# A new order of stages on all five engines of a two-layer transformer kernel

## The chip, the core and the metric

The kernel runs on one core of one Trainium2 chip. The metric is the device time of one execution in microseconds (us), as the median of several runs. Five engines run side by side, each taking its own instructions strictly in order: PE (TensorE, matrix products), ACT (ScalarE), DVE (VectorE), POOL (GpSimd) and SP (SyncE, which here only issues DMAs). They meet through semaphores.

## The reference

The input is 2 x 1024 rows of 256 features. With LN for a layer norm without weights, the reference computes

```
xn = LN(x);  x = x + attention0(xn) + ffn0(xn)
xn = LN(x);  x = x + attention1(xn) + ffn1(xn)
```

- attention0: causal attention over 1024 positions, 32 query heads and 8 key/value heads of 8 dimensions, with rotary position coding and biases.
- ffn0: gated GELU with fp8 operands, 256 to 2 x 1024 to 256.
- attention1: for each position, attention among its 16 heads of 16 dimensions, with a rotary coding.
- ffn1: gated SiLU, an RMS norm over 1024, and ternary weights that are quantized from the fp32 weights in groups of 64.

## The kernel before

The rows are cut into 16 tiles of 128, eight for each of the two sequences. For a tile n the work is a set of named stages, and each stage has a function on the engine that does it:

- **Front of attention0.** `ln0`, `rs0` (POOL), `xn`, then on PE `xnT` (transpose) and `qkv` (projection), `qkvc` (DVE), `rope`, `qr`, `q2` (POOL), `qh`, `qm` (ACT) and `q0`, `q1` (DVE), which split q and k into pieces of bf16, `qxT` (PE transposes) and `kTc`, `qTc` (DVE copies).
- **Quads.** A quad Q is one block of 128 keys for one half of the heads of a tile. There are 144 quads. `qk.Q` writes four banks of scores (`psS`), `exp.Q` is four activations of 128x512 that empty them into `Pt`, `mask.Q` (POOL) is run on diagonal blocks, and `pv.Q` sums into `psV`. `qk.Q+1` needs the banks that `exp.Q` has read. `S1` and `ex1` of the second attention use the same four banks.
- **Back of attention0.** `ob`, `obT`, `att`, `attT`, `attTc`, `wo0`, `xa`.
- **ffn0.** four `up` per tile, `g`, `fh`, `sq`, `th` (ACT), `ge1`, `ge3` (DVE), `down`, `yff`, `xf`.
- **Front of attention1.** `ln1`, `rs1`, `xn1`, `xn1T`, `xn1Tc`, two `qkv1` per tile, `qk1c`, `ro1`, `ro2`, `v1c`. Then SP writes the tile to memory (`vw`) and reads it back in another layout (`vr`, three DMAs into the single buffer `G3`), and PE transposes it twice (`gT`). `vr.n` waits until `PV1.n-1` has read `G3`.
- **attention1.** `gTq` (DVE), `gTk` (ACT), `S1`, `ex1` (ACT), `PV1`, `o1r`, `o1T`, `o1`; `ow` and `at1r` (SP) carry the result through memory, `at1T`, `at1Tc`, `wo1`, `yo`.
- **ffn1.** four `gu` per tile, `tg` (ACT), `sg`, `hh` (DVE), `ssq` (ACT), `ssm`, `rsg`, `hxa` (ACT), `hx` (DVE), two `hxT`, `hTc`, `dn1`, `yout`, and `out` (SP).
- **Weights.** `w8` casts the fp8 weights. `tc`, `ts`, `tsc`, `tm`, `tcs`, `td`, `tde`, `tr`, `tw` do the ternary quantization in six blocks. `sin` and `tab` make the angles of the second rotary coding. `vz`, `idc`, `cst`, `zero`, `gz` fill constants.

Nothing on the chip chooses the order of the work. A table `ORDER` (lines 45 to 183) holds one string per engine, and each engine walks its string and calls the stage functions:

```
for name, n in first_pass("pe"):
    run[name](n)
```

Every stage begins with its waits, `w.wait_ge(semaphore, count)`, whose counts follow from the stage number alone. An engine that stands at a wait runs nothing that is behind it in its string.

All PE stages other than `qk`, `pv` and `S1` write to one of three shared banks, psA, psB and psC, in rotation (`shared`). The bank is given by the place of the stage in the order of fills: a fill takes the bank of the third fill before it, and waits until that one has been emptied by the stage that `EMPTIED` names. There are 500 fills. So the order on PE also says which bank a stage gets and whose copy it waits for.

Of the kernel before, what the change touches and what calls it, by code (L numbers as in the profile page):

```python
# [46 lines left out]
        "xnT.0 qkv.0 xnT.1 ts.0 qkv.1 ts.1 qxT.0 qxT.1 qxT.2 qk.0 qk.1 td.0 up.0 up.1 xnT.2 qxT.3 pv.0 qkv.2 qxT.4 "  # L47
        "xnT.3 pv.1 qxT.5 obT.0 tr.0 up.2 qk.2 attT.0 qkv.3 up.3 td.1 up.4 qk.3 pv.2 up.5 qk.4 pv.3 qk.5 down.0 "
        "qxT.6 tr.1 qxT.7 up.6 qxT.8 up.7 pv.4 pv.5 qk.6 wo0.0 ts.2 up.8 ts.3 qk.7 pv.6 up.9 qxT.9 qxT.10 qk.8 pv.7 "
        "qxT.11 td.2 xnT.4 qk.9 td.3 tr.2 pv.8 pv.9 qk.10 tr.3 down.1 qkv.4 ts.4 obT.1 ts.5 qk.11 pv.10 attT.1 up.10 "  # L50
        "up.11 qk.12 wo0.1 up.12 td.4 qk.13 td.5 tr.4 up.13 tr.5 xnT.5 pv.11 xn1T.0 qkv.5 ts.6 obT.2 pv.12 qk.14 "
        "pv.13 attT.2 ts.7 qxT.12 qk.15 pv.14 down.2 qxT.13 qk.16 wo0.2 td.6 qxT.14 td.7 tr.6 qk.17 pv.15 pv.16 tr.7 "
        "qkv1.0 qkv1.1 ts.8 qk.18 ts.9 qxT.15 gu.0 up.14 qk.19 pv.17 pv.18 td.8 up.15 td.9 tr.8 up.16 tr.9 up.17 "
        "qk.20 pv.19 up.18 ts.10 down.3 ts.11 obT.3 up.19 qxT.16 qk.21 attT.3 xnT.6 pv.20 qk.22 pv.21 wo0.3 td.10 "
        "qk.23 td.11 tr.10 qxT.17 pv.22 qk.24 pv.23 tr.11 qkv.6 down.4 gu.1 qk.25 pv.24 gu.2 gu.3 qk.26 pv.25 xnT.7 "
        "xn1T.1 qk.27 pv.26 qkv1.2 gT.0 gT.1 qk.28 pv.27 S1.0 hxT.0 qkv1.3 hxT.1 qk.29 PV1.0 pv.28 qk.30 qxT.18 "
        "o1T.0 qxT.19 gu.4 qxT.20 qk.31 pv.29 gu.5 obT.4 gu.6 qk.32 at1T.0 attT.4 pv.30 wo0.4 wo1.0 gu.7 dn1.0 qk.33 "
        "pv.31 pv.32 qkv.7 qk.34 pv.33 xn1T.2 gT.2 gT.3 qk.35 pv.34 qkv1.4 qkv1.5 gu.8 gu.9 qk.36 pv.35 gu.10 gu.11 "
# [1585 lines left out]
```

## Time and profile before

| | us |
|---|---|
| median of 3 runs (684.7 to 686.87) | 685.07 |
| the profiled execution, its own time | 683.55 |
| its span, first to last instruction | 681.8 |
| PE busy | 609.7 (89%) |
| ACT busy | 502.1 (74%) |
| DVE busy | 450.6 (66%) |
| POOL busy | 279.4 (41%) |

The profiled execution is 1.5 us under the median. Its own time is 1.75 us above its span. The granted TensorE clock had a mean of 0.98 of full speed. A busy share says how long an engine ran something. It does not say what set the end; for that the waits of each stretch must be read.

### The profile page before, as it was taken

What the parts mean: (1) busy time and instruction counts of PE and PEld (TensorE: products, weight loads), DVE (VectorE), ACT (ScalarE), POOL (GpSimd) and SP (SyncE); (2) the same over time, 40 slices, a digit from 0 to 9 for tenths busy, and PEclk for the clock granted to TensorE, in tenths of its full rate; (3) what the DMA queues carried; (4) which work ended last, traced back from release to release, by engine and by line L of the source; (5) the groups of instructions that cost most, each with busy time, mean ns of one, the idle gap of its engine ahead of it and who ended that gap; (6) DMA issues with size and microseconds to landing.
All of it is one profiled execution on the core that took longest, in us unless ns stands there. A gap on an engine that the chain in (4) does not pass through costs nothing.

```text
span 681.8 us, 13961 instructions
## 1 busy us (share of the span) xinstructions
PE 609.7 (89%) x5206; PEld 305.7 (45%) x5245; DVE 450.6 (66%) x901; ACT 502.1 (74%) x941; POOL 279.4 (41%) x415
## 2 busy tenths in 40 slices
PE   2688988997999999999999998989999979998873
PEld 1244433443434455454545345654345524444552
DVE  5897988976556676847888965555537725536653
ACT  2559988985688986888789787478999848875330
POOL 6668575172333133634888561103144222312100
PEclk9999999999999999999999999999999979999997
DMA  8511010034000412312100114151021120043620
GB/s 280 197 56 32 32 32 1 1 48 63 9 24 24 63 19 38 39 18 47 40 1 1 47 19 57 29 80 30 25 25 17 39 39 25 25 70 40 91 42 20
DMA packets 150921, 30.47 MB, mean 45 GB/s; under 512 B 133952, under 2 KB 149568, under 8 KB 150848
## 3 DMA queue, kind: packets, MB, share of 16 engines
q1 hardware_dynamic: 150272, 29.19, 21.5%
q8 instruction: 43, 0.70, 0.4%
q10 hardware_dynamic: 576, 0.33, 0.2%
q14 instruction: 30, 0.25, 0.1%
HBM read 19.02 MB, written 10.49 MB: 43 GB/s over the span
## 4 chain that ended last, share of the span: by engine, by line
PE 46%; DMA 7%; DVE 6%; issue 3%; SPq 3%; ACT 2%; POOL 1%; DVEq 0%; POOLq 0%
PE psV L651 11%; PE psS L636 6%; DMA G<-qkvscr 3%; SPq L487 3%; DMA oscr<-o 2%; PE psS L754 2%; PE psB L819 2%; PE psC L800 2%; DMA at<-oscr 2%; PE psA L819 1%; PE psA L800 1%; PE psB L800 1%; ACT stage L935 1%; PE psC L765 1%; PE psA L765 1%
## 5 line engine op out<-in xcount | busy, mean ns | idle before, releaser
L887 ACT ACTIVATE Pt<-psS 128x512 f32<-128x512 f32 x576 | 300.0, 626 | 61.6 <-PE psS L636 43.0
L651 PE MATMUL psV<-Pt,vaug 128*32 128x512 f32 x1152 | 152.4, 611 | 1.7 <-POOL Pt L1507 1.0
L1507 POOL TENSOR_SCALAR_AFFINE_SELECT Pt<-Pt 128x512 f32<-128x512 f32 x128 | 86.9, 713 | 62.8 <-ACT Pt L887 62.6
L636 PE MATMUL psS<-qT,kT 49*128 49x512 bf16 x576 | 94.6, 388 | 4.7 <-ACT Pt L887 2.7
L636 PEld LDWEIGHTS psS<-qT,kT 49*128 49x128 bf16 x576 | 21.5, 94 | 63.4 <-ACT Pt L887 28.5
L651 PEld LDWEIGHTS psV<-Pt,vaug 128*32 128x32 f32 x1152 | 24.8, 109 | 51.2 <-issue 45.9
L935 ACT ACTIVATE stage<-psS 128x512 f32<-128x512 f32 x64 | 33.1, 606 | 15.9 <-PE psS L754 15.7
L1562 POOL TENSOR_TENSOR ss<-ss,mhalf 128x1 f32<-128x1 f32 x16 | 8.9, 554 | 79.9 <-DVE ss L1343 79.9
L1543 POOL TENSOR_TENSOR xhs<-xn1T,xhs 128x256 f16<-128x256 f32 x16 | 11.7, 729 | 52.8 <-DVE xhs L1260 52.8
L1208 DVE SCALAR_TENSOR_TENSOR gw<-gw,gb 128x512 f32<-128x512 f32 x32 | 24.7, 781 | 10.4 <-ACT gw L901 10.4
L1553 POOL TENSOR_TENSOR r<-qk,cos 128x256 f32<-128x256 f32 x16 | 14.6, 909 | 41.4 <-ACT qk L919 32.5
L1527 POOL TENSOR_TENSOR yfb<-yff,bo 128x256 f32<-128x256 bf16 x16 | 12.8, 799 | 45.3 <-DVE yff L1235 45.3
L1349 DVE SCALAR_TENSOR_TENSOR qtmp<-qtmp,ss 128x1024 f16<-128x1024 f32 x16 | 22.3, 1396 | 10.1 <-ACT qtmp L955 10.0
L950 ACT ACTIVATE qtmp<-qtmp 128x1024 bf16<-128x1024 f32 x16 | 17.2, 1073 | 13.9 <-issue 6.0
L1536 POOL TENSOR_SCALAR rs<-mv 128x1 f32<-128x1 f32 x16 | 6.2, 386 | 48.5 <-DVE mv L1243 48.5
L1217 DVE SCALAR_TENSOR_TENSOR ga<-gw,gb 128x512 bf16<-128x512 f32 x32 | 24.4, 763 | 1.1 <-ACT gw L912 1.0
L800 PE MATMUL psA<-wguT,xhs 128*128 128x512 bf16 x89 | 23.2, 380 | 0.9 <-issue 0.5
L912 ACT ACTIVATE gw<-gw 128x512 f32<-128x512 f32 x32 | 21.1, 668 | 3.2 <-DVE gw L1208 3.2
L1490 POOL TENSOR_TENSOR rt<-rt,QX 128x320 f32<-128x320 f32 x16 | 14.7, 916 | 20.2 <-ACT QX L873 15.8
L800 PE MATMUL psB<-wguT,xhs 128*128 128x512 bf16 x75 | 20.5, 390 | 1.9 <-issue 1.3
L754 PE MATMUL psS<-qk1T 24*128 24x128 f32 x512 | 20.8, 284 | 1.1 <-ACT qk1T L926 1.1
L901 ACT ACTIVATE gw<-gb 128x512 f32<-128x512 bf16 x32 | 21.4, 695 | 0.1
(355 smaller groups left out, 1363.2 us busy)
## 6 DMA issues: line engine op xcount, KB each, us to landing
qkvscr<-rqkv SPq DMA_DIRECT2D x16, 384.0 KB, 2.7
G<-qkvscr SPq DMA_DIRECT2D x48, 128.0 KB, 3.7
stage<-in_wg SPq DMA_DIRECT2D x4, 512.0 KB, 6.4
oscr<-o SPq DMA_DIRECT2D x16, 128.0 KB, 3.2
at<-oscr SPq DMA_DIRECT2D x16, 128.0 KB, 2.0
out<-yout SPq DMA_DIRECT2D x16, 128.0 KB, 1.7
x<-in_x SPq DMA_DIRECT2D x1, 1536.0 KB, 11.8
r<-in_wgu SPq DMA_DIRECT2D x2, 512.0 KB, 8.6
```

The lines of the kernel that those rows point to most:

```text
L636: e.matmul(psS[j][:], kT[64 * f:64 * f + 49, j, 128 * at:128 * at + 128], qd[64 * f:64 * f + 49, 4 * j:4 * j + 4, :].rearrange("p s n -> p ...
L651: ins = e.matmul(psV[32 * j:32 * j + 32, :], vaug[:, at, j, 32 * f:32 * f + 32], Pt[(4 * Q + j) % NP][:], start=(kb == 0 and h == 0), stop ...
L754: ins = e.matmul(psS[b][:, 128 * j:128 * j + 128], qk1T[32 * b:32 * b + k, 1, j, :], qk1T[32 * b:32 * b + k, 0, j, :], start=True, stop=True)
L800: ins = e.matmul(bank[:], src[:, pt, 128 * c:128 * c + 128], wguT[:, c, c0:c0 + 512], start=(k == 0), stop=(k == 3))
L887: e.activation(Pt[u % NP][:], psS[j][:], ACT.Exp, scale=SC0).then_inc(S["exp"], 1)
L901: e.activation(gw[:, half, :], gb[:, half, :], ACT.Square).then_inc(S["sq"], 1)
L912: e.activation(gw[:, half, :], gw[:, half, :], ACT.Tanh, scale=GC * GA).then_inc(S["th"], 1)
L935: e.activation(P1[:, 4 * b:4 * b + 4, :].rearrange("p g n -> p (g n)"), psS[b][:], ACT.Exp, scale=SC1).then_inc(S["ex1"], 1)
L1208: e.scalar_tensor_tensor(gw[:, half, :], gw[:, half, :], 1.0 / GA, gb[:, half, :], ALU.add, ALU.mult).then_inc(S["ge1"], 1)
L1217: e.scalar_tensor_tensor(a, gw[:, half, :], 1.0, gg, ALU.add, ALU.mult).then_inc(S["ge3"], 1)
L1349: e.scalar_tensor_tensor(hx_b[:, 1, :], h1, sn[:, 2:3], hx_b[:, 0, :], ALU.mult, ALU.subtract).then_inc(S["hx"], 1)
L1507: e.affine_select(out=p, in_=p, pattern=[[0, 4], [1, 128]], compare_op=ALU.is_ge, fill=0.0, base=0, channel_multiplier=-1).then_inc(S["mas ...
```

## The change

The five strings of `ORDER` are replaced. Each engine still runs exactly the same stages (804 on PE, 435 on ACT, 670 on DVE, 178 on POOL and 88 on SP), with the same functions and the same wait counts. 60 stages on PE, 47 on ACT, 18 on DVE, 18 on POOL and 25 on SP keep their place in the string. Since the place of a fill on PE gives its bank, the banks of the shared fills change with it. The core of the diff, the parts that the prediction speaks of:

```diff
     "pe": (
-        "xnT.0 qkv.0 xnT.1 ts.0 qkv.1 ts.1 qxT.0 qxT.1 qxT.2 qk.0 qk.1 td.0 up.0 up.1 xnT.2 qxT.3 pv.0 qkv.2 qxT.4 "
...
-        "xn1T.1 qk.27 pv.26 qkv1.2 gT.0 gT.1 qk.28 pv.27 S1.0 hxT.0 qkv1.3 hxT.1 qk.29 PV1.0 pv.28 qk.30 qxT.18 "
-        "o1T.0 qxT.19 gu.4 qxT.20 qk.31 pv.29 gu.5 obT.4 gu.6 qk.32 at1T.0 attT.4 pv.30 wo0.4 wo1.0 gu.7 dn1.0 qk.33 "
...
-        "hxT.21 qxT.47 qk.122 pv.121 o1T.10 qkv1.23 qk.123 down.15 pv.122 qk.124 pv.123 gu.44 qk.125 pv.124 at1T.10 "
...
-        "gu.55 o1T.12 gu.56 pv.143 gT.26 gT.27 obT.15 S1.13 gu.57 attT.15 gu.58 at1T.12 wo0.15 gu.59 wo1.12 PV1.13 "
-        "dn1.12 xn1T.15 hxT.26 o1T.13 qkv1.30 gT.28 gT.29 qkv1.31 S1.14 gu.60 hxT.27 PV1.14 at1T.13 o1T.14 gu.61 "
-        "gu.62 gu.63 gT.30 gT.31 S1.15 at1T.14 wo1.13 wo1.14 dn1.13 hxT.28 PV1.15 hxT.29 o1T.15 dn1.14 hxT.30 hxT.31 "
-        "at1T.15 wo1.15 dn1.15"),
+        "xnT.0 qkv.0 ts.0 xnT.1 xnT.2 ts.1 qkv.1 qxT.0 xnT.3 qxT.1 qxT.2 qkv.2 up.0 up.1 qk.0 up.2 qxT.3 qxT.4 qkv.3 "
+        "qk.1 qxT.5 td.0 td.1 qk.2 pv.0 up.3 tr.0 up.4 pv.1 qk.3 pv.2 tr.1 xnT.4 qxT.6 qxT.7 qk.4 obT.0 qxT.8 ts.2 "
...
+        "down.4 up.21 qxT.19 qxT.20 pv.29 qk.31 gu.4 o1T.0 pv.30 pv.31 qk.32 hxT.1 gu.5 gu.6 qk.33 gu.7 pv.32 qk.34 "
+        "obT.4 gu.8 pv.33 pv.34 qk.35 qkv1.4 qk.36 at1T.0 gT.2 qxT.21 pv.35 qk.37 pv.36 wo1.0 attT.4 qk.38 gT.3 "
...
+        "gT.26 gT.27 obT.15 gu.56 attT.15 S1.13 wo0.15 gu.57 PV1.13 gu.58 at1T.12 gu.59 xn1T.15 o1T.13 wo1.12 "
+        "qkv1.30 qkv1.31 gT.28 gT.29 hxT.26 S1.14 dn1.12 PV1.14 hxT.27 at1T.13 o1T.14 gu.60 wo1.13 gu.61 gu.62 "
+        "dn1.13 gT.30 gT.31 hxT.28 S1.15 gu.63 at1T.14 hxT.29 PV1.15 o1T.15 wo1.14 dn1.14 hxT.30 hxT.31 dn1.15 "
+        "at1T.15 wo1.15"),
     "act": (
-        "tc.0 sin.0 qh.0 qm.0 qh.1 exp.0 qm.1 exp.1 tde.0 g.0 fh.0 sq.0 th.0 g.1 exp.2 qh.2 sq.1 fh.1 qm.2 g.2 th.1 "
...
+        "tc.0 qh.0 qm.0 qh.1 g.0 qm.1 sq.0 fh.0 g.1 th.0 exp.0 sq.1 exp.1 tde.0 qh.2 tde.1 exp.2 g.2 sq.2 fh.1 qm.2 "
...
+        "sq.6 exp.14 th.6 sin.0 g.7 sq.7 fh.7 exp.15 tde.6 tde.7 exp.16 g.8 fh.8 qh.5 tc.4 qk1c.0 qm.5 exp.17 tg.0 "
...
     "dve": (
-        "vz.0 idc.0 ln0.0 xn.0 ln0.1 xnTc.0 ln0.2 xn.1 ln0.3 cst.0 qkvc.0 tab.0 xnTc.1 va.0 q0.0 w8.0 qkvc.1 q1.0 "
...
+        "ln0.0 vz.0 xn.0 ln0.1 ln0.2 xnTc.0 xn.1 ln0.3 idc.0 xn.2 qkvc.0 tsc.0 va.0 w8.0 xnTc.1 xnTc.2 tsc.1 q0.0 "
+        "w8.1 qkvc.1 xn.3 q1.0 tm.0 w8.2 kTc.0 xnTc.3 va.1 qTc.0 w8.3 qTc.1 q0.1 tcs.0 q1.1 qkvc.2 w8.4 va.2 ge1.0 "
...
     "pool": (
-        "zero.0 gz.0 rs0.0 rs0.1 rs0.2 rs0.3 rope.0 qr.0 q2.0 rope.1 qr.1 mask.0 q2.1 rs0.4 mask.1 rs0.5 rope.2 qr.2 "
...
+        "zero.0 rs0.0 rs0.1 rs0.2 rope.0 rs0.3 qr.0 q2.0 rope.1 qr.1 q2.1 rope.2 mask.0 mask.1 qr.2 rs0.4 q2.2 "
```

## Rows read from the trace of the kernel before

**Rows 1.** Page: span, busy time and share, granted clock by slices
```profile
span 681.8 us, 13961 instructions
PE 609.7 (89%) x5206; PEld 305.7 (45%) x5245; DVE 450.6 (66%) x901; ACT 502.1 (74%) x941; POOL 279.4 (41%) x415
PEclk9999999999999999999999999999999979999997
```

**Rows 2.** Busy time of each engine in five stretches: stretch, length, PE, PEld, DVE, ACT, POOL, clock
```profile
0.00:27.00 27.00, 10.09 (x34) 5.44 (x34) 16.71 (x43) 6.43 (x8) 15.68 (x34) 1.00 0.87 294
27.00:175.00 148.00, 130.67 (x975) 60.19 (x990) 121.39 (x229) 119.80 (x221) 83.74 (x121) 0.99 0.14 32
175.00:540.00 365.00, 352.90 (x3206) 179.84 (x3220) 241.65 (x485) 301.32 (x574) 153.19 (x221) 1.00 0.19 31
540.00:618.00 78.00, 73.04 (x572) 30.94 (x578) 34.96 (x69) 57.02 (x109) 22.06 (x33) 0.96 0.23 42
618.00:681.80 63.80, 42.99 (x423) 29.30 (x424) 35.88 (x78) 17.52 (x29) 4.73 (x8) 0.89 0.33 50
```

**Rows 3.** Waits of PE from 27 to 618 us: total, times, longest
```profile
PE psB L550 <- DMA at<-oscr: 6.0, 3, 3.8
PE psA L550 <- DMA at<-oscr: 4.6, 1, 4.6
PE psB L721 <- DMA G<-qkvscr: 2.8, 3, 1.6
PE psS L636 <- ACT Pt L887: 2.7, 2, 2.0
PE psC L721 <- DMA G<-qkvscr: 1.7, 1, 1.7
```

**Rows 4.** Chain that ended last, 440 to 475 us: start, us, what
```profile
448.65 1.85 PE psV L651 x16
472.72 0.54 PE psS L636 x4
473.26 0.99 PE psV L651 x8
```

**Rows 5.** Timeline of PE around at1T.0: start, us, instruction, idle before
```profile
169.40 0.33 PE L550 MATMUL psA<-identf,at 128*128 128x128 f32 x1 [4.59 <-DMA at<-oscr]
170.02 1.94 PE L651 MATMUL psV<-Pt,vaug 128*32 128x512 f32 x8
```

**Rows 6.** Timeline of ACT, table loads and the first exponential
```profile
11.94 1.28 ACT L851 ACT_TABLE_LOAD   x1
18.58 0.26 ACT L851 ACTIVATE sin<-ang 128x64 f32<-128x64 f32 x1 [5.36 <-DVE ang L1001]
28.15 1.28 ACT L887 ACT_TABLE_LOAD   x1
29.45 2.07 ACT L887 ACTIVATE Pt<-psS 128x512 f32<-128x512 f32 x4
```

**Rows 7.** Busy time of each engine in the slice from 68 us
```profile
68.20:102.30 34.10, 30.73 (x224) 13.52 (x220) 30.79 (x59) 30.74 (x58) 22.25 (x30) 1.00 0.10 32
```

**Rows 8.** Timeline of PE in the tail: pv.143, PV1.14, S1.15, o1T.15, at1T.15, dn1.15
```profile
618.88 1.07 PE L651 MATMUL psV<-Pt,vaug 128*32 128x512 f32 x8
641.87 1.08 PE L765 MATMUL psB<-stage,G 128*32 128x128 f32 x32 [0.78 <-ACT stage L935]
652.66 1.17 PE L754 MATMUL psS<-qk1T 24*128 24x128 f32 x32 [0.78 <-ACT qk1T L926]
659.96 0.66 PE L774 MATMUL psB<-identf,o1r 128*128 128x128 f32 x4 [0.26 <-DVE o1r L1312]
666.43 0.33 PE L550 MATMUL psC<-identf,at 128*128 128x128 f32 x1 [1.17 <-DMA at<-oscr]
668.47 3.47 PE L819 MATMUL psB<-wpT,stmp 128*128 128x256 bf16 x16
```

**Rows 9.** Timeline of DVE and ACT in the tail: last yout, ssq.15
```profile
671.97 0.42 DVE L1379 TENSOR_TENSOR yout<-psB,yo 128x256 f32<-128x256 f32 x1 [2.84 <-PE psB L819]
659.78 1.06 ACT L950 ACTIVATE qtmp<-qtmp 128x1024 bf16<-128x1024 f32 x1 [3.83 <-issue]
```

241 rows, old and new, of the table ORDER are left out of this document.

## Prediction

> **What bounds the kernel now.** I read the page first, then the busy times by stretch, then PE's waits, then the chain that ended last, and only then timelines of the places where PE stood. The page says that PE is busy 89% of the span and ACT 74% [rows 1], so PE is the engine whose idle time counts. The stretches say where it idles [rows 2]: 16.9 us of the first 27, 17.3 us of the next 148, only 12.1 us of the 365 after that, 5.0 us from 540 to 618, and 20.8 us of the last 63.8. The reader is to see that the middle is nearly full and that the head, the first quarter and the tail are not. The order matters only where PE stands still or runs its matmuls at the lower clock.
>
> PE's waits from 27 to 618 us name the cause there [rows 3]: 10.6 us for the DMA that brings `at1` back (`at1T`) and 4.5 us for the DMA that fills `G3` (`gT`), 15.1 us together. The next one, scores that wait for `exp`, is 2.7 us. Two of the waits are long, 4.6 us before `at1T.0` and 3.8 us before `at1T.10`. What follows such a wait is slow too: the `pv` behind `at1T.0` took 1.94 us [rows 5], against 0.99 for one in a dense stretch [rows 4]. So a wait of 4.6 us cost PE nearly another 1 us in that `pv` alone.
>
> **The change, part by part.** No instruction is added or removed in the text of the stages, so each term is a wait that goes, one that comes, or work that moves under something else.
>
> *Round trips through memory in the middle.* I counted, in the two PE strings, the work that lies between `o1T.n` and `at1T.n`, weighing each stage with its slot at full clock (0.54 us for a `qk`, 0.99 for a `pv` [rows 4], and likewise for the others, between 0.25 and 1.8). For `at1T.0` before, this is qxT, gu, qxT, qk, pv, gu, obT, gu, qk, or 6.0 us. Behind the new order stand 13.8 us. Over the sixteen tiles, fifteen gaps before are 7.3 us or shorter, and fifteen after are 8.3 us or longer. The trip itself is short when nothing else is in the way: from the end of `o1T.15` (659.96 + 0.66 = 660.6) to `at1T.15` at 666.4 it is 5.8 us [rows 8]. The same count between `PV1.n-1` and `gT.2n` gives seven gaps of 3.3 to 5.2 us before and none under 6.4 after. So the new order covers both trips in nearly every tile. If all of the 15.1 us [rows 3] went, and with them some 3.5 us of slow matmuls behind the waits (my estimate from four slots like the one in [rows 5], each 0.65 to 1.0 us over its dense length), the gain would be 18.6 us. The other bound is 0: in a program with in-order queues a wait that is covered often shows up at the next late copy. The work that is now put between producer and consumer has to be ready too, and ACT and DVE are busy for 80% and more of the second stretch [rows 2]. I take a little over half, **-10 us**, because the middle has other slack (DVE 66%, ACT 83% of the third stretch) but the second stretch has not.
>
> *Tail.* Before, the last `pv` ends at 619.9, `S1.15` starts at 652.7 and the last `yout` ends at 672.4: 32.8 and 19.7 us [rows 8, 9]. In the new string the projection `qkv1.30 qkv1.31` stands directly behind `wo1.12`, no longer behind `dn1.12`, and not split by `gT.28 gT.29`. Counting slots and the copies between them from `pv.143` on, I get `qkv1.31` some 5 us earlier, and `PV1.14` ending 20 us after `pv.143` in place of 23 (641.87 + 1.08 = 642.95 [rows 8]). `vr.15` waits for `PV1.14`; with some 6 us for the trip, `gT.30` can run at 26 and `S1.15` at 27.4 instead of 32.8, 5.4 us earlier. Behind `S1.15` the old string has `at1T.14 wo1.13 wo1.14 dn1.13 hxT.28` ahead of `PV1.15`, 5.4 us after `S1.15` starts, while `ex1.15` is done after 3.3. The new one has `gu.63 at1T.14 hxT.29`, so `PV1.15` starts at about 3.3. `hxT.29` also releases `ssq.15`, which began only at 659.8 [rows 9], 7.1 us after `S1.15`. And `dn1.15` now comes ahead of `at1T.15`. In the old order it ran last and alone, at the lower clock, in 3.47 us [rows 8]. My count of this last piece gives 15.0 to 16.6 us where 19.7 stood, the second value with `dn1.15` still slow. Together that is 8.5 to 10.1 us. It needs ACT and DVE to be prompt, which they can be: they are busy for 17.5 and 35.9 us of these 63.8 [rows 2]. As lower bound I keep 3, the gain behind `S1.15` alone. I take **-8 us**. The checks behind the last `yout`, some 9 us to the end of the span, are the same.
>
> *Head.* `sin` no longer stands between `tc.0` and `qh.0`; there ACT waited 5.36 us for the angles [rows 6]. `gz` goes out of the way of `rs0.0`, and `cst` and `tab` out of the way of the copy of the first projection. Each of the first steps becomes ready 1 to 2 us earlier. But `w8.1` to `w8.3`, `tm.0` and two `up` now come ahead of `qk.0`, and by my count `qk.0` starts where it did, at about 27 us, with `qkv.2`, `xnT.2`, `xnT.3`, `up.0` and `up.1` done (2.7 us of slots more). I take **-2 us**, with +1 if the weights land later than counted and -5 if the second stretch profits as well.
>
> *Sine in the busy stretch.* `sin.0` now stands between `th.6` and `g.7`, behind `exp.14`. Its own two activations are 0.5 us. A load of 1.28 us preceded `sin` and another the first exponential [rows 6]; now the tanh and exponentials on both sides want a table other than that of `sin`, so I count two loads there, 2 x 1.28 + 0.5 = 3.1 us of ACT, in the slice where ACT is busy for 30.7 of 34.1 us [rows 7]. That is the upper bound, 0 the lower, if PE has other work. I take **+1.5 us**. The Trainium skill speaks against this move more strongly (ScalarE: Activation LUTs, What ACT_TABLE_LOAD costs): every switch to another set costs the load and a drain of the same length, some 2.66 us. By that page the move would cost ACT 5.8 us and the sum would be 1.3 us higher. The trace does not show such a drain: the exponential starts at 29.45, right behind the load that began at 28.15 and lasted 1.28 [rows 6].
>
> *Pairs.* Two adjacent `pv` take 1.85 us where two single ones take 1.98 [rows 4]. The number of such neighbours on PE rises from 17 to 38, which is worth at most 21 x 0.13 = 2.7 us; stages that alternate between fp32 and narrower operands cost a little and rise from 405 to 416. I take **-1 us** (bounds 0 and -2.7).
>
> The sum is -10 - 8 - 2 + 1.5 - 1 = -19.5 us. Against the profiled execution's own 683.55 this gives 664.05; the median of the runs stands 1.5 us above that execution, so I predict **665.6 us**.
>
> **Rivals.** *All of it comes* (chance 0.17): every covered wait is really gone, 18.6 in place of 10, tail 10, head 3, pairs 2, no cost for the sine: 683.55 - 33.6 + 1.5 = about 651, and up to 659 if one of them falls short. For it speaks the regularity of the new gaps; against it that ACT and DVE fill up where PE does.
>
> *Only the ends come* (0.20): the waits for the two DMAs go, but PE then waits for copies and exponentials at the same pace, since the second stretch is held by ACT. Then tail and a part of the head remain, 5 to 11 us, or 671 to 682, about 677. For it speaks that the 12.1 us of idle in the third stretch are spread thinly.
>
> *Nothing changes* (0.05): every gain is handed back; 683 to 687.
>
> *Slower, by the three shared banks* (0.08): each of the 497 fills behind the first three waits for the copy of the third fill before it. I counted the PE work between the two: it is under 1.5 us for 98 fills before and for 119 after. Where DVE has something else ahead of that copy (one more 128x512 operation is 0.7 us), PE stands. If the new DVE string meets the short gaps 0.3 us worse on average, 119 x 0.3 = 36 us come back, and the kernel runs at 685 - 19.5 + 36 = about 701. This decides from 0.17 us per short gap on (20/119). Against it: the fewest-slack gaps, below 1.2 us, fall from 55 to 49.
>
> **How the numbers follow.** The forecast, 659 to 671, has a chance of 0.50. The range reaches into the rivals on both sides, down to 655 and up to 679; outside lie half of the first rival and a good part of the last three, 0.2 in all. A change of less than 0.3% (2 us) can't be told from none in this kernel. Faster by more than that: 0.50 + 0.17 + 0.20 = 0.87. Within it: 0.05. Slower: 0.08.
>
> **What the changed profile would show.** PE's waits from the first quad to `pv.143` would have at most 3 us for the DMAs of `at1` and `G3` together, and no `pv` of 1.9 us. `pv.143` would end near 610. From its end to `S1.15` would be 27 to 30 us, and from there to the last `yout` 15 to 17. ACT would have four table loads, two of them around `sin` near 85 us, each with no more than 0.1 us of idle behind it. I would be wrong by the second rival if PE's idle in the second and third stretch stayed near 29 us with other names in the list of waits, and by the last if waits of psA, psB and psC for DVE grew by more than 10 us.

## The result and the profile after

| | before | after |
|---|---|---|
| median of the runs, us | 684.88 (4 runs, 684.34 to 686.87) | 646.5 (4 runs, 643.59 to 648.37) |
| ratio | | 0.9431, 95% interval 0.9386 to 0.9476 |
| the profiled execution, its own time | 683.55 | 643.59 |
| span | 681.8 | 641.8 |
| PE busy, idle | 609.7, 72.1 | 592.7, 49.1 |

The new order is 38.4 us faster. That is twice what was forecast (19.5), and below the range. The profiled executions differ by 40.0 us, which is the number that the readings below add up to; the one of after is the fastest of its four. The page of after answers to [rows 1]:

```profile
span 641.8 us, 13919 instructions
PE 592.7 (92%) x5195; PEld 304.4 (47%) x5245; DVE 437.3 (68%) x901; ACT 498.0 (78%) x941; POOL 275.3 (43%) x415
PEclk9799999999999999999999999999999999999997
```

PE's idle time fell by 23.0 us and its busy time by 17.0, though it runs the same instructions. A reader who looks only at the idle time misses much of the gain. The split is not exact: these two traces lack records of matmuls (5206 and 5195 of the 5245 that there are, most of the missing ones `gu`, 28 and 41), and a missing record shows as idle time or lengthens its neighbour. Where a split between busy and idle matters below, two traces that have all 5245 decide. The busy time by stretch answers to [rows 2] (columns: stretch, length, then PE, PEld, DVE, ACT, POOL, clock, DMA share, GB/s):

```profile
0.00:27.00 27.00, 10.99 (x39) 5.89 (x40) 16.14 (x40) 5.00 (x6) 15.55 (x31) 0.91 0.88 300
27.00:175.00 148.00, 136.31 (x1074) 62.00 (x1086) 124.62 (x238) 135.05 (x254) 90.39 (x129) 0.99 0.14 31
175.00:500.00 325.00, 321.29 (x2930) 167.03 (x2955) 213.14 (x443) 272.06 (x523) 134.93 (x203) 1.00 0.21 34
500.00:578.00 78.00, 77.02 (x648) 35.82 (x653) 43.16 (x93) 65.97 (x128) 25.73 (x40) 1.00 0.20 35
578.00:641.80 63.80, 47.10 (x514) 33.69 (x513) 40.19 (x90) 19.94 (x34) 8.71 (x14) 0.93 0.38 62
```

From 27 to 175 us PE idles 11.7 us where it idled 17.3, and ACT is busy for 135.1 us where it was for 119.8: it does more of its work early, and the stretch that I took to be held by ACT got shorter even so. From 175 to 500 the idle time is 3.7 us, from 500 to 578 it is 1.0. The waits of PE from 27 us to the last `pv` answer to [rows 3] (total, times, longest). These are the largest; no wait for the DMAs of `at1` or `G3` is in the list:

```profile
PE psA L599 <- POOL QX L1501: 1.5, 1, 1.5
PE psC L566 <- DVE qkv L1100: 1.2, 1, 1.2
PE psV L652 <- POOL Pt L1508: 0.8, 2, 0.6
PE psB L567 <- DVE qtmp L1052: 0.8, 2, 0.5
```

PE around `at1T.0` ([rows 5] before, with 4.59 us of idle and a `pv` of 1.94 us behind it). There is no idle in brackets now, and what follows the first `pv` starts 1.00 us behind it, the second `pv` 0.54 behind the `qk`, both dense:

```profile
170.45 0.33 PE L551 MATMUL psB<-identf,at 128*128 128x128 f32 x1
...
171.47 1.06 PE L652 MATMUL psV<-Pt,vaug 128*32 128x512 f32 x8
172.47 0.61 PE L637 MATMUL psS<-qT,kT 49*128 49x512 bf16 x4
173.01 1.07 PE L652 MATMUL psV<-Pt,vaug 128*32 128x512 f32 x8
```

ACT's table loads ([rows 6]) and `sin`, now in the busy stretch:

```profile
2.76 1.28 ACT L859 ACT_TABLE_LOAD   x1 [2.76 <-issue]
...
91.13 1.28 ACT L852 ACT_TABLE_LOAD   x1
92.42 0.26 ACT L852 ACTIVATE sin<-ang 128x64 f32<-128x64 f32 x1
...
94.56 1.28 ACT L888 ACT_TABLE_LOAD   x1
95.86 1.57 ACT L888 ACTIVATE Pt<-psS 128x512 f32<-128x512 f32 x3
```

The tail on PE and DVE answers to [rows 8, 9]: the last `pv` (two in one record), `S1.15`, `dn1.15`, `at1T.15`, the last `yout`:

```profile
585.08 1.92 PE L652 MATMUL psV<-Pt,vaug 128*32 128x512 f32 x16
616.64 1.17 PE L755 MATMUL psS<-qk1T 24*128 24x128 f32 x32 [0.33 <-DVE qk1T L1296]
627.39 1.91 PE L820 MATMUL psC<-wpT,stmp 128*128 128x256 bf16 x16 [1.36 <-DVE yout L1380]
629.14 0.27 PE L551 MATMUL psA<-identf,at 128*128 128x128 f32 x1
```
```profile
631.72 0.42 DVE L1380 TENSOR_TENSOR yout<-psC,yo 128x256 f32<-128x256 f32 x1
```

From the end of the last `pv` (587.0) to `S1.15` are 29.6 us (32.7 before), from there to the end of the last `yout` (632.1) 15.5 (19.7 before). `dn1.15` takes 1.91 us and no longer 3.47, since the granted clock is 1.00 there until 633 us; in the old order it was 0.5 from 668.2 to 671.6.

**Three stretches tell the whole difference.** Cut both executions at the first quad and at the end of the last `pv`. Before, and then after:

```profile
0.00:27.10 27.10, 10.09 (x35) 5.48 (x36) 16.81 (x43) 6.43 (x8) 15.78 (x34) 1.00 0.87 294
27.10:619.95 592.85, 558.56 (x4762) 271.31 (x4798) 399.01 (x785) 479.68 (x907) 259.01 (x375) 0.99 0.18 33
619.95:681.80 61.85, 41.05 (x410) 28.92 (x413) 34.76 (x74) 15.98 (x27) 4.61 (x8) 0.89 0.31 49
```
```profile
0.00:30.00 30.00, 13.99 (x58) 7.59 (x58) 18.56 (x43) 5.91 (x7) 17.11 (x32) 0.89 0.87 293
30.00:587.00 557.00, 540.61 (x4727) 268.92 (x4772) 384.35 (x784) 475.78 (x908) 253.81 (x377) 1.00 0.19 33
587.00:641.80 54.80, 38.12 (x414) 27.92 (x417) 34.35 (x75) 16.34 (x27) 4.38 (x7) 0.92 0.34 60
```

The first quad starts 2.9 us later, but 3.9 us more of PE's work lies ahead of it, so the head gives 1.0. The tail gives 7.05. (The start of the first quad differs between executions of one and the same head: 26.0 to 29.1 us in the ten traces with the old one, middle 26.9, and 30.0 to 32.4 in the eight with the new one, middle 31.6. The 30.0 is the earliest of its kind. By the middles the new head starts the quads 4.7 us later with some 4 us more work done, which is no gain.) The stretch between is 35.85 us shorter: 17.9 of idle and 17.95 of busy time, 3.9 of the latter being the work that moved ahead. What the other 14 us of busy time are, and which part of the order took the idle time away, the experiments have to tell.

One part stands in the clock. In the old order the granted clock fell to half (1.2 of 2.4 GHz) three times in this stretch, each time at a wait of PE for one of the two DMAs: the wait of 4.59 us that ended at 169.40, one of 1.74 for `G3` that ended at 425.95, and the one of 3.81 that ended at 550.44. Before, the three stretches:

```profile
169.90:173.30 3.40, 3.40 (x13) 1.38 (x12) 0.76 (x2) 1.21 (x3) 0.00 (x0) 0.50 0.00 0
425.90:429.30 3.40, 3.35 (x15) 2.19 (x15) 1.12 (x2) 1.72 (x3) 0.00 (x0) 0.50 0.35 65
548.80:555.60 6.80, 5.16 (x18) 1.21 (x18) 1.11 (x2) 2.07 (x4) 1.52 (x3) 0.50 0.14 25
```

PE is busy for 11.9 us of them at half pace, which costs an estimated 6 us. After, the granted clock is 1.00 from 29 to 633 us. (The 1.00 of the first row of before counts the time ahead of the first record of the clock as full; `qk.0` at 27.09 us took 1.03 us and one behind `at1T.0` in the new order 0.61, so the clock was low there too.)

### The profile page after: what moved, and what is told of

It is laid out like the page before. It is cut to its first block and busy times, and to the rows that moved or that the text cites. A ratio compares the mean times of both kernels' runs of the same rounds, so it can differ in the third digit from the quotient of the medians.

```text
span 641.8 us, 13919 instructions
## 1 busy us (share of the span) xinstructions
PE 592.7 (92%) x5195; PEld 304.4 (47%) x5245; DVE 437.3 (68%) x901; ACT 498.0 (78%) x941; POOL 275.3 (43%) x415
## 5 line engine op out<-in xcount | busy, mean ns | idle before, releaser
L888 ACT ACTIVATE Pt<-psS 128x512 f32<-128x512 f32 x576 | 298.5, 621 | 37.8 <-PE psS L637 29.7
L652 PE MATMUL psV<-Pt,vaug 128*32 128x512 f32 x1152 | 146.1, 601 | 1.8 <-POOL Pt L1508 0.8
L1508 POOL TENSOR_SCALAR_AFFINE_SELECT Pt<-Pt 128x512 f32<-128x512 f32 x128 | 87.5, 721 | 54.7 <-ACT Pt L888 54.5
L637 PE MATMUL psS<-qT,kT 49*128 49x512 bf16 x576 | 96.7, 382 | 1.8 <-ACT Pt L888 0.5
L652 PEld LDWEIGHTS psV<-Pt,vaug 128*32 128x32 f32 x1152 | 26.5, 108 | 54.6 <-issue 41.7
L1477 POOL TENSOR_TENSOR rt<-qkv,cs 128x320 f32<-128x320 f32 x16 | 14.9, 930 | 37.4 <-DVE qkv L1100 36.8
L1218 DVE SCALAR_TENSOR_TENSOR ga<-gw,gb 128x512 bf16<-128x512 f32 x32 | 26.4, 824 | 4.6 <-ACT gw L913 4.6
L874 ACT ACTIVATE QX<-rt 128x768 bf16<-128x768 f32 x16 | 14.0, 876 | 15.0 <-PE psB L599 9.5
L1500 POOL TENSOR_TENSOR QX<-rt,QX 128x256 bf16<-128x256 f32 x16 | 12.0, 750 | 29.7 <-ACT QX L880 22.3
L1209 DVE SCALAR_TENSOR_TENSOR gw<-gw,gb 128x512 f32<-128x512 f32 x32 | 23.3, 729 | 0.8 <-ACT gw L902 0.8
L1544 POOL TENSOR_TENSOR xhs<-xn1T,xhs 128x256 f16<-128x256 f32 x16 | 12.5, 782 | 26.1 <-DVE xhs L1261 26.1
L801 PE MATMUL psB<-wguT,xhs 128*128 128x512 bf16 x84 | 22.2, 379 | 1.3 <-issue 0.6
L1221 DVE TENSOR_TENSOR ga<-ga,fb 128x512 bf16<-128x512 bf16 x32 | 18.7, 586 | 5.1 <-ACT fb L908 1.5
L1480 POOL TENSOR_TENSOR rt<-qkv,sn 128x160 f32<-128x160 f32 x32 | 22.1, 713 | 0.0
L951 ACT ACTIVATE qtmp<-qtmp 128x1024 bf16<-128x1024 f32 x16 | 17.3, 1079 | 5.5 <-issue 5.5
```

The source lines that it names most:

```text
L637: e.matmul(psS[j][:], kT[64 * f:64 * f + 49, j, 128 * at:128 * at + 128], qd[64 * f:64 * f + 49, 4 * j:4 * j + 4, :].rearrange("p s n -> p ...
L652: ins = e.matmul(psV[32 * j:32 * j + 32, :], vaug[:, at, j, 32 * f:32 * f + 32], Pt[(4 * Q + j) % NP][:], start=(kb == 0 and h == 0), stop ...
L801: ins = e.matmul(bank[:], src[:, pt, 128 * c:128 * c + 128], wguT[:, c, c0:c0 + 512], start=(k == 0), stop=(k == 3))
L888: e.activation(Pt[u % NP][:], psS[j][:], ACT.Exp, scale=SC0).then_inc(S["exp"], 1)
L1209: e.scalar_tensor_tensor(gw[:, half, :], gw[:, half, :], 1.0 / GA, gb[:, half, :], ALU.add, ALU.mult).then_inc(S["ge1"], 1)
L1218: e.scalar_tensor_tensor(a, gw[:, half, :], 1.0, gg, ALU.add, ALU.mult).then_inc(S["ge3"], 1)
```

## The experiments

Each median stands beside runs of the kernel before on the same chip (medians 683.4 to 684.9 us). "Trips" are the two ways through memory, `ow` and `at1r` to `at1T`, and `vw` and `vr` to `gT`.

### One third of the order at a time

Three kernels take the new order on all five engines for a part of the work and the old one for the rest. They are cut at `qk.30` and `pv.138` in PE's string, and each other engine at what these need.

```diff
 e1: -[old to qk.30]  +[the same stages in new order]   [old from there]
 e2:  [old to qk.30]            -[old to pv.138]  +[new order]    [old from there]
 e3:  [old to pv.138]           -[old to the end] +[new order]
```

Head alone (e1):

> The stages that the old order runs up to qk.30 (with the copies that empty their banks) stand in the relative order of the new one; all later stages stand as in the old order. If the gains of the stretches simply add up, this gives what the new kernel had gained at qk.30, 5 to 7 us. If the new head only pays because of what the new middle does with it, the gain is under 3 us.

683.72 us, ratio 0.999 (0.9962 to 1.0018): no change to be seen. In the trace it is 3.1 us ahead at `qk.30`, and then loses them at the cut. PE's waits from 150 to 195 us:

```profile
PE psB L595 <- POOL QX L1497: 4.6, 1, 4.6
```

Middle alone (e2):

> Only the stages from qk.30 to pv.138 stand in the relative order of the new string; head and tail are old. If the gains add up, the middle alone gives 23 to 28 us. If the middle's gain needs the head's (work that crosses the cut), it is under 18 us.

668.08 us, ratio 0.9758 (0.971 to 0.9806). At `qk.138` it is 26.0 us ahead, and from there to `qk.143` it needs 29.3 us where 17.4 stood before. 6.6 of the 12 us lost at this cut are two waits. Waits of PE from 560 to 620 us:

```profile
PE psB L718 <- DMA G<-qkvscr: 6.6, 2, 4.4
```

Tail alone (e3):

> Only the stages behind pv.138 stand in the new relative order. By the count of the tail the gain is 6 to 9 us; if the tail's latency is the DMAs' own, under 3 us.

680.08 us (10 runs), ratio 0.9936 (0.9908 to 0.9964). The middle holds most of the gain, the tail 4.7 us by the medians and 7.35 in the traces (61.85 to 54.5 us from the last `pv` to the end). The profiled execution of this kernel was the fastest of its ten, 5.3 us under their median. A spliced order costs something at its cut, so these three are rather lower bounds.

### The trips in the old order

In the first kernel (e4) `at1T.n` transposes the result of tile n-1, so that it never waits for its own trip; in the second (e5) `gT` transposes a constant weight as well. All DMAs are still issued, but the second attention's output goes to the wrong tile, and with `gT` changed its scores are made from other numbers.

```diff
-                w.wait_ge("d_or", 16 * (n + 1))
-                transpose_pair(shared("at1T", n), at1[n % len(at1)], "at1T")
+                w.wait_ge("d_or", 16 * n)
+                transpose_pair(shared("at1T", n), at1[(n + 1) % 2], "at1T")
...
-                w.wait_ge("d_vr", 48 * (n + 1))
-                transpose_groups(shared("gT", m), s, "gT")
+                w.wait_ge("d_c", 96)
+                ins = e.transpose(bank[:, 128 * j:128 * j + 128], wo0_w[...], identf[:])
```

> The old order, but at1T transposes the attention result that came back for the tile before (a second buffer, zeros for tile 0), so its output is left wrong in the second attention; all DMAs and stages remain, and only the wait for the tile's own round trip is gone. Theory 1, a covered wait is gone for good and takes the slow matmuls behind it along: 12.4 us of waits and 2 to 5 us behind them, so 13 to 18 us faster. Theory 2, it shows up again at the next late copy: 4 to 8 us. Theory 3, the trips are not what the new order gained by: under 4 us.

662.98 us, ratio 0.9709 (0.9656 to 0.9762): 21.8 us faster, for 12.4 us of waits that the old trace puts down to this DMA in the whole kernel, and more than the 13 to 18 of the best theory.

> The old order with both waits for round trips gone: at1T takes the result of the tile before, and gT transposes a constant weight tile in place of the tile that the DMA brings, so the scores of the second attention are left wrong; all DMAs and stages remain, and PV1 still waits for its data. Theory 1, covered waits are gone for good: 19 to 25 us faster than before. Theory 2, half of it comes back elsewhere: 9 to 13 us. Theory 3, the trips matter little: under 6 us.

659.06 us, ratio 0.9635 (0.959 to 0.9681): 25.9 us faster. The three stretches of this kernel, to be read against those of before:

```profile
0.00:29.10 29.10, 9.83 (x36) 5.50 (x37) 16.92 (x43) 6.42 (x8) 16.02 (x35) 0.83 0.82 275
29.10:600.50 571.40, 553.46 (x4763) 269.89 (x4800) 397.52 (x785) 478.47 (x907) 258.69 (x375) 0.99 0.19 34
600.50:658.30 57.80, 39.30 (x410) 28.13 (x413) 34.56 (x74) 15.84 (x27) 4.59 (x8) 0.91 0.34 53
```

From the first quad to the last `pv` it is 21.45 us shorter than before: 16.35 us of idle and 5.1 of busy time. The busy part is matmuls at half the clock behind a wait: the three stretches at 0.50 above are not in this trace, where the granted clock is 1.00 from 39.8 to 623.5 us. In the tail the trips are worth 4.05.

The same on the new order (e6):

> The same two changes on the new order. Theories 1 and 2: the new order has no such waits left before the tail, so it is within 3 us of the new kernel (646.5), the tail's last trip apart. If the new order still hides waits that only look like others, it gains 5 us or more.

646.05 us, ratio 0.9438 (0.939 to 0.9485), no different from the new order as it is. The new order has covered the trips wholly.

### Distance on PE, or the place in SP's string

In the old order something held the trips up that my count of PE's work did not contain. SP issues its DMAs in order too. Its queue in the old kernel, from 153 to 172 us: `vw.1`, `vr.1` (three), `ow.0`, `at1r.0`.

```profile
157.41 0.36 SPq L479 DMA_DIRECT2D qkvscr<-rqkv  x1
160.56 2.55 SPq L487 DMA_DIRECT2D G<-qkvscr  x3
163.16 1.38 SPq L492 DMA_DIRECT2D oscr<-o  x1
167.38 0.33 SPq L498 DMA_DIRECT2D at<-oscr  x1
```

The result of tile 0 was complete on DVE at 159.40, but `ow.0` went out at 163.16: it stood behind `vr.1`, which itself waited until `vw.1` had landed and then took 2.55 us to issue. So the trip of `at1T.0` was 3.8 us longer than a trip. The same holds for `at1r.10`, issued at 547.30 behind `vw.11 vr.11`, while its data had gone out at 540.46 and the median `ow` lands 3.2 us after its issue, so some 3.6 us late. These are the two long waits of [rows 3]. The new string has `vw.1 ow.0 at1r.0 vr.1` and `ow.10 at1r.10 out.9 vw.11 vr.11`. The old order with these three DMAs moved and nothing else (e9):

```diff
-        "vw.0 vr.0 vw.1 vr.1 ow.0 at1r.0 out.0 ...  ow.10 vw.11 vr.11 at1r.10 out.10 ..."
+        "vw.0 vr.0 vw.1 ow.0 at1r.0 vr.1 out.0 ...  ow.10 at1r.10 vw.11 vr.11 out.10 ..."
```

> The old order on all engines; on SP only three DMAs are moved: ow.0 and at1r.0 ahead of vr.1, and at1r.10 ahead of vw.11 and vr.11. In the old trace o1.0 is done at 159.4 us and ow.0 is issued at 163.2, behind vr.1, which waits for its own tile's write; at1r.10 is issued at 547.3 behind vr.11 where the write for it had landed near 543.6. Theory A, the two long waits of PE (4.6 and 3.8 us) are SP's queue: 3.7 us each go, and with the slow matmuls behind them 7 to 13 us. Theory B, it is the distance on PE that counts: under 3 us.

672.59 us, ratio 0.9826 (0.9794 to 0.9858): some 11 us from three moved DMAs. SP and PE there:

```profile
160.70 0.36 SPq L489 DMA_DIRECT2D oscr<-o  x1
164.97 0.33 SPq L495 DMA_DIRECT2D at<-oscr  x1
```
```profile
167.07 0.33 PE L547 MATMUL psA<-identf,at 128*128 128x128 f32 x1 [0.99 <-DMA at<-oscr]
```

`at1T.0` waits 0.99 us, no longer 4.59. The whole new string on SP and the old order elsewhere (e10):

> The old order on four engines with the whole new string of SP. Theory A: at least the gain of the three moved DMAs, and up to 3 us more from the shorter waits. Theory B: under 3 us; a wait that the new SP string brings (an out or an at1r ahead of a vw that PE needs) would make it less than the three DMAs alone.

674.6 us, ratio 0.9875 (0.9847 to 0.9903), 2 us less than the three DMAs alone gave; the two intervals overlap. Now the other way round, the new order with `ow.0 at1r.0` behind `vr.1` on SP (e15):

> The new order on all engines, but on SP's string ow.0 and at1r.0 stand behind vr.1 again, as in the old one. Theory A (the distance on PE covers the hold too: 13.8 us of work between o1T.0 and at1T.0 against a trip of some 6 us plus a hold of 3.7): at most 2 us slower than the new order, and at1T.0 waits less than 1 us. Theory B (the new place in SP's string is needed as well): 5 us or more slower, and at1T.0 waits 3 us or more.

645.78 us, ratio 0.9431 (0.9388 to 0.9474): nothing lost, and `at1T.0` does not wait. The number is that of theory A, the reason is not. SP's queue in this kernel:

```profile
153.36 0.36 SPq L476 DMA_DIRECT2D qkvscr<-rqkv  x1
155.89 2.54 SPq L484 DMA_DIRECT2D G<-qkvscr  x3
160.73 0.36 SPq L489 DMA_DIRECT2D oscr<-o  x1
```

`vr.1` is done at 158.4, before `ow.0` has anything to write, so it holds nothing up: from `vw.1` to `ow.0` are 7.37 us here, and 7.37 in the new order (150.28 to 157.65). The new order on the other engines puts `o1T.0` late enough behind `vw.1` for the hold to vanish by itself. Whether the distance on PE would cover a hold was therefore not tested. (`at1r.10` can't stand behind `vr.11` in the new order: `vw.11` needs `ro2.11`, which DVE's new string has behind `at1Tc.10`, so SP, PE and DVE would wait for each other. The second hold and the whole old SP string were therefore not tried with the new order.) And the new order with thirteen of the `at1T` drawn near their `o1T` (e7):

```diff
- ... o1T.0 pv.30 pv.31 qk.32 hxT.1 gu.5 gu.6 qk.33 gu.7 pv.32 qk.34 obT.4 gu.8 pv.33 pv.34 qk.35 qkv1.4 qk.36 at1T.0 ...
+ ... o1T.0 pv.30 pv.31 qk.32 hxT.1 gu.5 gu.6 qk.33 gu.7 pv.32 at1T.0 qk.34 obT.4 gu.8 pv.33 pv.34 qk.35 qkv1.4 qk.36 ...
```

> The new order, but at1T.n (n = 0 to 6 and 9 to 14) and its copy are drawn forward to 6.6 to 7.9 us of PE work behind o1T.n, the old distance; nothing else is moved. Theory 1: the waits for the DMA and the slow matmuls behind them come back, 8 to 16 us slower than the new kernel, 655 to 662. Theory 3: under 3 us slower.

659.0 us, ratio 0.9633 (0.9586 to 0.9679): 12.5 us slower than the new order, with 8.4 us of waits for this DMA in the whole kernel (two waits have 4.6 of it), and the granted clock at 0.50 from 249.6 to 253.0 us. The shared banks of the moved stages changed too; PE's waits for fills are 10.6 us, against 9.3 in the new order. So the new string on SP does not cover the trips by itself; the distance on PE is needed as well. SP's three DMAs alone gave 11 of the 26 us that the trips cost in the old order.

### Do trips, tail and head add up?

The old order to `pv.138`, the new one behind it, and both trips away (e14):

> The old order up to pv.138, the new one behind it, and both waits for round trips taken away on PE (at1T takes the result of the tile before, gT transposes a constant). It asks whether trips and tail add up, and how much is then left for the rest of the new order. The trips alone gave -25.9 us in the old order, the tail alone -4.7; the tail holds up to 3.3 us of waits for the trips that both remove. Theory (trips and tail are two separate gains, and head and middle beyond the trips are small): 654 to 658 us against 684.9. Rival (the rest of the new order in the middle is worth more than the trips leave it, so the two overlap): no faster than 659, the time of the trips alone.

658.57 us, ratio 0.9614 (0.9565 to 0.9662). The tail adds nothing that can be measured to the 659.06 of the trips alone. So the two are not separate gains: from the last `pv` to the end the old order needs 61.85 us, 57.8 with the trips away, 54.5 with the new tail and 55.5 with both. The last `pv` is not at the same place in the work, though, so the count from `qk.138` to the end is the fairer one: 84.7 us in the old order, 80.1 with the trips away, 81.0 with both, 80.4 in the new order. Most of what the new tail gives is the two last trips, covered.

With the new head as well (e16):

> New order up to qk.30 and behind pv.138, old order between, and both waits for round trips taken away on PE. It asks what the new order of the middle is worth beyond the trips. The head part alone gave -1.0 us in the old middle, because the join behind qk.30 ate a lead of 3.1 us. Theory (the middle is worth little beyond the trips): within 2 us of the kernel with trips and tail, so 652 to 657. Rival (the lead of the head is kept once the trips do not stop PE behind it): 650 to 653, 3 us or more below the kernel with trips and tail.

668.74 us, ratio 0.9786 (0.9737 to 0.9835), 10 us slower than without the new head. It has the same wait of 4.6 us for `QX` at its cut as the head alone, and starts its first quad 4.6 us later. 2.5 us and more of the 10 lie outside the span, since its own times stand 4.2 us and more above it where all others stand 1.7 to 1.9 above. At `qk.30` it is still 2.2 us ahead of the kernel without the new head and at `qk.138` 8.0 behind. This kernel tells what a bad seam costs, not what the head is worth; the question it was to answer stays open.

### The head of the new order

DVE stood 4.23 us in the new head, at `w8.2` for its weights, and `kTc.0` and `qxT.2` behind it:

```profile
24.54 0.69 DVE L1015 CAST w8g<-stage 128x1024 fp8e4<-128x1024 f32 x1 [4.23 <-DMA stage<-in_wg]
25.15 0.42 DVE L1130 COPY kT<-psB 128x512 bf16<-128x512 bf16 x1
```

The first variant (e12) puts `w8.2 w8.3` behind `qTc.1`, `qk.0` behind `qxT.2` and `exp.0` ahead of `g.0`. The second (e13) also puts the angles and `sin` back into the head (`tab.0` behind `q1.1`, `sin.0` behind `exp.0`).

```diff
- ... qxT.1 qxT.2 qkv.2 up.0 up.1 qk.0 up.2 ...
+ ... qxT.1 qxT.2 qk.0 qkv.2 up.0 up.1 up.2 ...
```

> The new order with w8.2 and w8.3 behind qTc.1 on DVE, qk.0 directly behind qxT.2 on PE and exp.0 ahead of g.0 on ACT. In the new trace DVE stands 4.2 us at w8.2 for its weights while the copy kTc.0 behind it is ready, and holds qxT.2 and qk.0. If that stall is on the path, qk.0 starts near 25 us in place of 30 and 2 to 5 us remain at the end; if the second stretch, where ACT is busy over 90%, sets the pace from other work, under 1 us.

> The same with tab.0 behind q1.1 on DVE and sin.0 behind exp.0 on ACT, so that both table exchanges fall where ACT is idle. If the 4 us that the kernel without sine gained are the exchanges in the busy stretch, 2 to 4 us faster than the kernel with the changed head alone; if tab.0 (4 us of DVE) now delays the second tile, no gain or a loss of 1 to 2 us.

643.57 us, ratio 0.9416 (0.9391 to 0.9441), and 644.62, ratio 0.9435 (0.9409 to 0.9461): neither can be told from the new order. In e12 `qk.0` starts at 25.4 us, 4.6 earlier, and at `qk.24` 1 us of that is left: 9.5 us of PE's work lie ahead of it where 14.0 did. So the start of the first quad alone is a poor mark of progress. And e13, with the sine back in the head, was to be 2 to 4 us faster than e12 and is not (644.62 against 643.57).

### The sine

The new order with both `sin` activations made scaled copies, which need no other table (e8; the second rotary coding is then wrong):

```diff
-                e.activation(sin1[:]..., ang[:, 0, :], ACT.Sin)
+                e.activation(sin1[:]..., ang[:, 0, :], ACT.Copy, scale=0.3)
```

> The new order with the two sine activations replaced by scaled copies, so the angles of the second rotary coding are left wrong and no table needs to be exchanged. If the two loads of 1.28 us in the busy stretch are on the path, 1.5 to 2.6 us faster than the new kernel; if PE has other work there, no difference.

642.41 us, ratio 0.9391 (0.9346 to 0.9436). The nearest comparison on the same chip is the new order without trips, 646.05: the sine costs 3.6 us here, and every run of the one was below every run of the other. That is the price of having the sine in the kernel, not of its place. The place was changed by e13 alone, together with `tab.0`: back in the head it gave nothing.

### The 12 us between the trips away and the new order

Old order, trips away: 659.06. New order: 646.5. Their stretches from the first quad to the last `pv` differ by 14.4 us. 1.5 of it is idle, 12.85 is busy time, and of that 3.9 us is work moved ahead of the first quad. So 9 us of PE's work is denser with no wait in it. Two traces without missing records, e14 (trips away, old order to `pv.138`) and e15 (new order but for one place on SP), say the same of the whole kernel:

```profile
PE 608.2 (93%) x5245; PEld 304.4 (46%) x5245; DVE 448.4 (68%) x901; ACT 500.6 (76%) x941; POOL 279.5 (43%) x416
PE 599.0 (93%) x5245; PEld 305.1 (47%) x5245; DVE 437.5 (68%) x901; ACT 498.1 (77%) x941; POOL 274.6 (43%) x415
```

Of these 9.1 us the clock explains an estimated 4.2. Up to the last `pv`, e14 has PE busy for 17.45 us at a granted clock of 0.50 (16.8 to 37.3 us and 590.2 to 593.6), e15 for 9.15 (21.4 to 31.6 and 41.9 to 45.3); half of the difference is 4.2.

I suspected neighbours for the rest: `pv` directly ahead of a `qk` or another `pv` takes a mean slot (its start to the start of the next stage) of 0.94 us, ahead of another stage 1.00; and `pv` followed by one of the two are 37 of 140 in the old order and 90 in the new. That mean mixes two things. By the medians, and alike in both orders, a `pv` ahead of another `pv` takes 0.88 us, ahead of a `qk` 0.99 to 1.00, ahead of any other stage 1.00. Only pairs of `pv` are shorter, by 0.115 us, and their number rises from 17 to 38: 2.4 us. The three kernels that follow were built on the mixed figure. They move only `pv`, only on PE. No fill passes another, so banks stay. In the first (e17) the pairs rise by one, so it can't show what pairs are worth.

```diff
-  qk.60 pv.59 qxT.24 qxT.25 at1T.3 qk.61 pv.60 qxT.26 wo1.3 qk.62 dn1.3 hxT.8 S1.4 pv.61 pv.62 qxT.27 hxT.9 qk.63
+  qk.60 qxT.24 qxT.25 at1T.3 pv.59 qk.61 qxT.26 wo1.3 pv.60 qk.62 dn1.3 hxT.8 S1.4 qxT.27 hxT.9 pv.61 pv.62 qk.63
```

> The old order with one thing changed, on PE alone: 80 of the pv that stand ahead of one to three other stages and then a qk or pv are moved behind those, directly ahead of that qk or pv. No fill moves against another fill, so the banks stay. The number of pv that are followed by a qk rises from 20 to 94. It asks what neighbours on PE are worth. In three executions of the old order a pv ahead of a qk or pv takes a slot of 0.94, ahead of another stage 1.00; a gu behind a qk takes 0.65, behind a pv 0.74. Theory N (the new order gains from neighbours beside the waits): 80 x (0.06 to 0.15) = 5 to 12 us faster than 684. Rival (slots of stages only shift time from one record to the next, the total is the same): within 3 us of 684, or slower if the later pv holds back exp.

712.24 us, ratio 1.0399 (1.0356 to 1.0442): 28 us slower. There is no gain from a `qk` behind a `pv`. The slots of the `pv` do sum to 4.2 us less, but a slot holds the wait of the next stage too; without the waits the `pv` take 1.2 us more than before. And something else costs the 28 us. (The expectation's 0.65 and 0.74 us for a `gu` come from traces that lack some of its records: in e14 and e15 no whole `gu` takes under 0.86.) The `exp` group of ACT before and in this kernel (busy and mean ns, then idle time ahead of it and what ended it):

```profile
L887 ACT ACTIVATE Pt<-psS 128x512 f32<-128x512 f32 x576 | 300.0, 626 | 61.6 <-PE psS L636 43.0 <-PE psV L651 18.4
```
```profile
L884 ACT ACTIVATE Pt<-psS 128x512 f32<-128x512 f32 x576 | 299.4, 622 | 96.7 <-PE psS L633 61.7 <-PE psV L648 34.7
```

A later `pv` frees `Pt` later, ACT's `exp` waits for it (18.4 to 34.7 us), scores and everything behind them on ACT come late, and PE stands at the fills (9.5 to 23.3 us). Of the 28 us between the first quad and the last `pv`, 17.8 are idle and 10.05 busy time.

> The same move of 80 pv, with both waits for round trips taken away as well, as in the kernel that gave -25.9 us. Theory N: 5 to 12 us below 659, so 647 to 654, which closes most of the gap to the new order's 646.5. Rival: 656 to 662.

684.0 us, ratio 0.9999 (0.9974 to 1.0023): 25 us slower than the trips away alone, the same price. Without the trips' waits the late `pv` (this is e18) costs as much as with them.

> The other way round: the new order with 39 of its pv moved to an earlier place on PE, directly behind the qk ahead of them, so that pv followed by a qk fall from 52 to 29 and adjacent pairs of pv from 38 to 22. Fills keep their order. Theory N: 39 x (0.06 to 0.15) = 2 to 6 us slower than 646.5. Rival: within 1.5 us of it.

650.42 us, ratio 0.95 (0.9471 to 0.9528), 3.9 us slower than the new order (e19). The stretch from the first quad to the last `pv`:

```profile
32.00:594.80 562.80, 544.10 (x4729) 268.83 (x4771) 383.48 (x782) 475.89 (x907) 252.82 (x376) 1.00 0.19 32
```

5.8 us longer than in the new order, 3.5 of it busy and 2.3 idle time. Of the busy part, 16 pairs less at 0.115 us are 1.8, and 1.7 is the clock: from 100.4 to 103.8 us PE is busy throughout at a granted clock of 0.50, which the new order has nowhere between 29 and 633 us. So the kernel agrees with pairs as the only neighbours that count, and its result was in theory N's range partly by luck. The new order has ACT's `exp` waiting less than the old one, 37.8 us in all and 7.5 for `Pt`:

```profile
L888 ACT ACTIVATE Pt<-psS 128x512 f32<-128x512 f32 x576 | 298.5, 621 | 37.8 <-PE psS L637 29.7 <-PE psV L652 7.5
```

## Why the prediction was wrong

**The round trips in the middle: the failed step is "I take a little over half, -10 us".** The measured size of the term is -21.45 in the trace (e5 against before, first quad to last `pv`), above even the bound of 18.6. The mechanism was right, and so was the count of gaps. I took the half because "a wait that is covered often shows up at the next late copy"; it did not. The waits of PE for fills, other than for these DMAs, sum to 9.5 us before and 9.3 after. The bound itself was short in two ways. I allowed 3.5 us for slow matmuls behind the waits, and 5.1 were there. I had the 3.5 from single slots, and from one that was read against another measure (1.94 us as a record stands against 1.06, not 0.99). The granted clock shows the whole: 11.9 us of busy time at 0.50 behind three of the waits, in which all matmuls are slow and not only the first. And 15.1 us of waits were named in [rows 3], while 16.35 of idle went: removing a wait also moves everything behind it.

**What the prediction did not see** is SP's string. It named the gap on PE for `at1T.0`, 6.0 us, and a free trip of 5.8, and then did not ask why a trip of 5.8 made PE wait 4.6. The answer stood in SP's queue. It would have told that those two waits, 8.4 us by their longest in [rows 3], had a cause of their own, worth 11 us in e9. The new SP string moves both DMAs ahead, which the prediction could have read in the strings, so that a discount on them made no sense. For the first of them e15 shows that the new order on the other engines removes the hold as well.

**Tail, -8.** Right: 7.05 in the trace (7.3 of them up to `yout`, from 32.7 + 19.7 to 29.6 + 15.5), each part in the interval that the prediction named, and `dn1.15` at full pace. The run of it alone showed 4.7. But it is no separate term beside the trips, since 4.05 of it are the last trips, and from `qk.138` to the end the gain is 4.3 us and not 7.05: the new order does some of the tail's work ahead of the last `pv`.

**Head, -2.** 1.0 in the trace by the sum of start and work done, and about nothing by the middle of all traces with either head; the first quad at 30.0 and not at 27, held by `w8.2` and its weights. It lies inside the bounds of +1 and -5; no experiment separated it.

**Sine, +1.5, with 0 to 3.1.** The term is the price of moving the sine, and only e13 against e12 bears on it: with the sine in the head 1.05 us slower, within the noise, and with `tab.0` moved too. So the move cost nothing that can be measured, the lower bound. The 3.6 us of e8 is what the sine costs where it stands now, against no sine at all; what it cost in the old head no run shows. I counted four loads, and three are there: the first one, at 2.76, already serves the functions before `sin`, so the number is as before. The Trainium skill (ScalarE: Activation LUTs, What ACT_TABLE_LOAD costs) has 2.66 us for a switch with a drain in it, an estimate of 5.3 for two switches. The trace shows no drain, as before: `sin` starts at 92.42, right behind the load of 91.13 + 1.28. ACT loses 3.1 us there by the rows, and without the sine PE gains about as much.

**Pairs, -1, with 0 to -2.7.** By the slots, 21 more pairs at 0.115 us are 2.4, inside the bounds. What the sum lacked is another term: PE's work between the first quad and the last `pv` is 9 us denser than in the old order with the trips away (553.46 to 540.61, less 3.9 moved ahead), and the prediction put what lies beyond trips and pairs at nothing. By e14 and e15 some 4 of the 9 are time at the lower clock, more than half of it in the first 45 us, and 2.4 are pairs. The other 2.5 or so stay open. It is not `gu`: its 256 matmuls take 59.6 us in e14 and 59.1 in e15, each counted from its start to the next matmul's start or its own end.

In sum, in the trace: head -1.0, trips -21.45, denser work -9.0, other idle time -1.5, tail -7.05, together -40.0. What the sine costs is inside the terms of the middle.

**The rivals.** "All of it comes" (0.17) was the nearest, at 651: waits, slow matmuls and tail all came. The range was drawn to leave half of it out, at 655, and the denser work on PE took the time 4.5 us past its centre. "Only the ends come" is refuted by its own sign, PE's idle time in the second and third stretch: 16.0 us from 27 to 540 us where 29.4 stood, and not with other names; e4 and e5 agree. "Slower, by the three shared banks" is refuted for this order by the waits for fills, 9.5 and 9.3 us. ACT's late `exp`, by which e17 got slower by 28 us (with 23.3 us of waits for fills behind it), was in none of my rivals.

## What to carry to other kernels

When PE waits for a DMA, compare the trip's length with the work on PE that should cover it. If the wait is more than the difference, look in the queue of the engine that issues the DMA for one that waits there for something else. Three DMAs moved ahead of such a one gave 11 us.

Price a removed wait with all matmuls behind it that ran at the lower clock: read the granted clock of the stretch behind each wait, not one slot. Take a discount only where a row shows the next late producer.

Before you add up busy times of two traces, compare their counts of instructions with what the program issues, and before you take a mean slot, look at its classes one by one.

When an order of stages is changed, place `pv` (what frees the buffers of the busy second engine) by that engine's need first: 80 of them moved one to three stages later cost 28 us.

## What the hardware showed that was not expected

- PE's busy time for the same instructions depends on their order. With all records there, it is 608.2 us in e14 and 599.0 in e15, and an estimated 4.2 of the 9.1 us are time at the lower clock. Two adjacent `pv` (eight fp32 matmuls each) save 0.115 us; a `qk` behind a `pv` saves nothing.
- A wait costs PE more than its length, by what follows it: in the old order the granted clock stood at 0.50 in three stretches at and behind waits of 4.59, 1.74 and 3.81 us, for 13.6 us in all. From the first quad to the last `pv`, 16.35 us of idle went with 5.1 us of busy time, a factor of 1.3. The medians give more: 12.4 us of waits for `at`, 21.8 us gained (e4).
- One queue's in-order issue made a trip longer by 3.8 us, and another by some 3.6, with no mark in the waits of PE other than the name of the DMA.
